# Shared-key attention: key tiles summed four at a time on GpSimd before the ones product

## The chip, the cores and the metric

The kernel runs on one core of one Trainium2 chip. The metric is the device time of one execution in microseconds (us). Five engines work side by side and meet only at semaphores: TensorE (PE, with its weight loads shown apart as PEld), VectorE (DVE), ScalarE (ACT), GpSimd (POOL) and SyncE (SP), which issues most DMAs.

## The reference

Two sandwich layers on a sequence of 2 x 2048 tokens of 128 values: local attention, a feed-forward layer, causal attention, a second feed-forward layer. The change lies in the attention inside the first feed-forward layer. It has four query heads of 32 dimensions that share one set of keys and values, over all 2048 tokens of a batch:

```
Q = (nx @ Wq.T).reshape(B, S, H, dk).transpose(0, 2, 1, 3)
Kc = nx @ Wkc.T
Vc = nx @ Wvc.T
scores = jnp.einsum('bhsd,btd->bhst', Q, Kc) * scale
attn = jax.nn.softmax(scores, axis=-1)
out = jnp.einsum('bhst,btd->bhsd', attn, Vc)
```

The softmax needs for each query and head the sum of 2048 exponentials. That sum is what the change works out in another way.

## The kernel before

The function is mqa_attention, L761 to L1253. The queries of a batch are cut into 8 units of 256 (UQ); there are 16 units, U0 to U7 in batch 0 and U8 to U15 in batch 1. The 2048 keys are cut into 16 tiles of 128 (KT), taken two at a time; gi = 0 to 7 counts these pairs within a unit.

For each unit and each key tile:
- TensorE multiplies keys with the four heads' queries (scores, L1170) into PSUM.
- ScalarE takes the exponential (L1049) into one of six slots of the ring pt: 128 keys by 4 heads by 256 queries. It waits until the slot's last readers are done: the values product of tile T - 6 and the GpSimd add that read it (sums_with, L830, counts the adds that must be done).
- TensorE multiplies values with the exponentials (values, L1181), four matmuls of 32 columns each, one a head, adding up in the bank pvb.
- For the denominators, GpSimd adds the exponentials of two tiles (L1089) into one of three buffers psum, seven such pair sums a unit. TensorE then multiplies a matrix of ones with each pair sum (sums, L1189), again four matmuls, adding up in the other half of pvb. The last two tiles of a unit are not added first: TensorE multiplies ones with each of them (last_sums, L1196). That is nine products with ones a unit.

Before a unit's exponentials can be taken, its row maxima must be known. They are found a unit or two ahead, in 32 passes (first_pass, L1154, with VectorE's maximum at L914), laid between the other work by the tables EARLY, LATE and ALL. At gi = 5 (TURN) VectorE closes the next unit's maxima in top (L917): a reduction over the 32 partial maxima (L919), a cast of the result into the tile mt (L924) and a subtraction for its low part (L926). TensorE waits for these and turns mt round (max_rows, L1160), and ScalarE and VectorE copy the rows out (L1025, L931). Ahead of max_rows TensorE projects the queries of the unit after the next (project, L64 to L66). Unit U6 of a batch has no such projection, and U7 has neither passes nor maxima.

At the end of a unit (close, L1201) TensorE does the last two values products, the last pair sum and last_sums. ScalarE then evacuates pvb (L1032), TensorE turns it (L1211), and VectorE divides (post, L939 and L941). The first scores of a unit are queued on TensorE behind the close of the one before.

The order on each engine is that of the code. On TensorE at each gi: two scores, at gi = 5 the projection and max_rows, some passes, the values of the pair before, the pair sum of gi - 2, some passes. Between units some engines do other small work: VectorE statistics, weights or normalised rows for the next stage (L716 to L724, L1874, L1883, L963), GpSimd powers (L735, L1078) and two subtractions (L1895). S.stats and later are these helpers.

Of the kernel before, what the change touches and what calls it, by code (L numbers as in the profile page):

```python
# [9 lines left out]
ALU = mybir.AluOpType  # L10
# [718 lines left out]
def stats_pool(nc, pool, S, rows=slice(0, 2), chunks=range(4)):  # L729

    n = rows.stop - rows.start
    for c in chunks:
        tiles = slice(c * S.CT, (c + 1) * S.CT)
        pool.wait_ge(S.step, 1 + (c + 1) * S.chunk_steps)
        nc.gpsimd.tensor_tensor(S.rs[:, rows, tiles], S.ve[:, rows, tiles],  # L735
                                S.half[:, 0:n * S.CT].rearrange("p (a b) -> p a b", b=S.CT),
                                ALU.pow).then_inc(S.powed, 1)
# [10 lines left out]
KT = SEQ // P  # L748
# [4 lines left out]
RING = 6  # L753
UQ = 256
UT = UQ // P
SUMS = 3
PAIR_SUMS = KT // 2 - 1
GRP = 4


def mqa_attention(nc, dr, X, g, S, wq, wkv, ao, later, x2):  # L761

    m = Mem(nc, "b1_")
    with m:
# [8 lines left out]
        pt = m.sb("pt", [P, RING, HB, UQ])  # L773
        psum = m.sb("psum", [P, SUMS, HB, UQ])
# [33 lines left out]
        summed = m.sem("summed")  # L808
        den_mm = m.sem("den_mm")
        st_mm = m.sem("st_mm")  # L810
        exp_done = m.sem("exp_done")
# [17 lines left out]

        def sums_with(T):  # L830

            return T // KT * PAIR_SUMS + min(T % KT // 2 + 1, PAIR_SUMS)

        def block_of(U):
            return U % UNITS
# [9 lines left out]
        def passes_at(u, g, half):  # L845

            if g >= TURN:
                return (u + 2, EARLY[g][half]) if u + 2 < UNITS else (None, 0)
            if u + 1 >= UNITS:
                return None, 0  # L850
            return u + 1, (ALL if u == 0 else LATE)[g][half]

        with nc.Block() as block:
# [210 lines left out]
            @block.gpsimd  # L1064
            def _(pool):
                nc.gpsimd.memset(ones[:, :], 1.0).then_inc(zeroed, 1)
                nc.gpsimd.memset(mt[:, :, :], 0.0).then_inc(zeroed, 1)
                pool.wait_ge(zeroed, 2)
                nc.gpsimd.memset(ks[QROWS:QROWS + 2, :].bitcast(F32), 1.0).then_inc(zeroed, 1)
                pool.wait_ge(zeroed, 3)  # L1070

                def between(U):
                    if U in (2, 3):
                        stats_pool(nc, pool, S, rows=slice(1, 2), chunks=(U,))
                    if U in (4, 5):
                        half = slice(BT * (U - 4), BT * (U - 3))
                        pool.wait_ge(S.step, 1 + S.CHUNKS * S.chunk_steps)
                        nc.gpsimd.tensor_tensor(S.r[:, half], S.ve[:, 0, half], S.half[:, half], ALU.pow).then_inc(r_done, 1)  # L1078
                    if U in (6, 7):
                        later.low2(nc, pool, U - 6)  # L1080

                for U in range(BATCH * UNITS):
                    between(U)
                    for k in range(PAIR_SUMS):
                        T, n = U * KT + 2 * k, U * PAIR_SUMS + k
                        pool.wait_ge(exp_done, T + 2)
                        if n >= SUMS:
                            pool.wait_ge(den_mm, n - SUMS + 1)
                        nc.gpsimd.tensor_tensor(psum[:, n % SUMS, :, :], pt[:, T % RING, :, :], pt[:, (T + 1) % RING, :, :],  # L1089
                                                ALU.add).then_inc(summed, 1)  # L1090

            @block.tensor
            def _(pe):
# [19 lines left out]
                def load(b):  # L1113
                    turn_in(b, 0)
                    turn_in(b, 1)
                    for i in range(BB):
                        n = b * BB + i
                        cols = slice(i * BLK, (i + 1) * BLK)
                        if i + 2 < BB:
                            turn_in(b, i + 2)  # L1120
                        pe.wait_ge(xh_ready, n + 1)
                        pe.wait_ge(xl_ready, n + 1)
                        if i >= 2:
                            pe.wait_ge(k_lo, n - 1)
                        matmul_split(nc, p1b[:, i % 2, :], wkv[0][:, :], wkv[1][:, :], xh[:, cols],
                                     xl[:, cols]).then_inc(kv_mm, 1)
                        if i > 0:
                            turn_values(b, i - 1)
                    turn_values(b, BB - 1)
                    pe.wait_ge(k_lo, (b + 1) * BB)  # L1130
                    pe.wait_ge(v_ready, (b + 1) * BB)
# [25 lines left out]
                def max_rows(V):  # L1157
                    pe.wait_ge(m_split, V * 2 + 2)
                    for t in range(UT):
                        last = nc.tensor.transpose(misc[:, t * P:(t + 1) * P], mt[:, t, :], ident[:, :])  # L1160
                    last.then_inc(mt_mm, 1)
# [13 lines left out]
                def values(U, i):  # L1175
                    T = U * KT + i
                    if i == 0 and U > 0:
                        pe.wait_ge(post_done, U)
                    pe.wait_ge(exp_done, T + 1)
                    for h in range(HB):  # L1180
                        last = nc.tensor.matmul(pvb[h * DK:(h + 1) * DK, 0:UQ], v1[:, i, :], pt[:, T % RING, h, :],  # L1181
                                                start=(i == 0), stop=(i == KT - 1), skip_group_check=True)
                    last.then_inc(pv_mm, 1)

                def sums(U, k):
                    n = U * PAIR_SUMS + k
                    pe.wait_ge(summed, n + 1)
                    for h in range(HB):
                        last = nc.tensor.matmul(pvb[h * DK:(h + 1) * DK, UQ:2 * UQ], ones[:, :], psum[:, n % SUMS, h, :],  # L1189
                                                start=False, stop=False, skip_group_check=True)  # L1190
                    last.then_inc(den_mm, 1)

                def last_sums(U):
                    for i in (KT - 2, KT - 1):
                        for h in range(HB):
                            last = nc.tensor.matmul(pvb[h * DK:(h + 1) * DK, UQ:2 * UQ], ones[:, :],  # L1196
                                                    pt[:, (U * KT + i) % RING, h, :], start=False, stop=(i == KT - 1),
                                                    skip_group_check=True)
                    last.then_inc(den_last, 1)

                def close(U):  # L1201
                    values(U, KT - 2)
                    values(U, KT - 1)
                    sums(U, PAIR_SUMS - 1)
                    last_sums(U)

                def post(U):
# [7 lines left out]
                for b in range(BATCH):  # L1215
                    load(b)
                    V = b * UNITS
                    project(V)
                    for r in range(P1):
                        first_pass(V, r)  # L1220
                    max_rows(V)
                    project(V + 1)
                    done = [0] * UNITS
                    for u in range(UNITS):
                        U = V + u

                        def passes(g, half):
                            w, count = passes_at(u, g, half)
                            for _ in range(count):
                                first_pass(V + w, done[w])  # L1230
                                done[w] += 1

                        for gi in range(PAIRS_OF_TILES):
                            if gi == 0 and u > 0:
                                close(U - 1)
                            scores(U, 2 * gi)
                            scores(U, 2 * gi + 1)
                            if gi == TURN and u + 2 < UNITS:
                                project(U + 2)
                            if gi == TURN and u + 1 < UNITS:  # L1240
                                max_rows(U + 1)
                            passes(gi, 0)
                            if gi == 0 and u > 0:
                                post(U - 1)
                            if gi > 0:
                                values(U, 2 * gi - 2)
                                values(U, 2 * gi - 1)
                            if gi > 1:
                                sums(U, gi - 2)
                            passes(gi, 1)  # L1250
                    close(U)
                    post(U)
                    pe.wait_ge(post_done, (b + 1) * UNITS)  # L1253
# [2215 lines left out]
```

## Time and profile before

| | us |
|---|---|
| Median of 3 runs | 2171.54 |
| Lowest and highest run | 2165.57, 2171.64 |
| Profiled execution, first to last instruction (span) | 2116.7 |
| The two together: the median less the span | 54.8 |

The page gives the profiled execution's own time as its span, 2116.7 us; the time of a run also holds what lies around the span. Busy shares of the span:

| Engine | busy us | share |
|---|---|---|
| TensorE matmuls | 1765.5 | 83% |
| TensorE weight loads | 1331.8 | 63% |
| VectorE | 1492.7 | 71% |
| ScalarE | 974.9 | 46% |
| GpSimd | 923.7 | 44% |

A matmul of float32 data shows as two records, so the four matmuls of one product with ones are eight records. Matmuls are pipelined and their ends modelled, so the distance from one start to the next says more than a duration. The granted clock of TensorE is 1.00 at 2.4 GHz and 0.50 at 1.2 GHz. The stage that changes runs from 640 to 1177 us of the span, with the loading of batch 1 in the middle (884 to 933).

### The profile page before, as it was taken

The page shows a single profiled execution, that of the slowest core. Times are in us where ns is not written, and L with a number is a line of the kernel's source. Part 1 is how long each engine was busy: PE and PEld are TensorE (multiplying, and loading weights), DVE is VectorE, ACT ScalarE, POOL GpSimd, SP SyncE. Part 2 cuts the span into 40 slices and gives each one's busy share as a digit, 9 for nine tenths or more (in the row PEclk, how much of TensorE's full clock was granted, in tenths as well). Part 3 has the DMA queues.
Part 4 walks back from the last instruction along what each step waited for, and adds up shares of the span by engine and source line. Part 5 has one row for each costly group of instructions (what it writes and reads, how often), then busy time and mean ns, then how long its engine had stood idle before and what let it go on. Part 6 is the DMA issues. An engine that isn't in the chain of part 4 may idle for free. (4 is left out here: it accounts for less than half of the span.)

```text
span 2116.7 us, 37485 instructions
## 1 busy us (share of the span) xinstructions
PE 1765.5 (83%) x13932; PEld 1331.8 (63%) x13932; DVE 1492.7 (71%) x3418; ACT 974.9 (46%) x2147; POOL 923.7 (44%) x637
## 2 busy tenths in 40 slices
PE   3788888888769999889999779965899779978993
PEld 2677777777635666446665557644688558767883
DVE  5678777787477887387787478878787776864234
ACT  2455545545415565525556345432333244325664
POOL 3455555565314566514555336654000220165644
PEclk9999999999859999979999889988899889988997
DMA  5112112111010000000000023319600000016763
GB/s 172 66 63 81 51 71 76 56 71 66 16 42 1 2 1 1 1 1 1 1 2 1 1 71 101 95 60 229 149 1 1 0 1 1 8 38 194 213 219 118
DMA packets 78469, 124.11 MB, mean 59 GB/s; under 512 B 11824, under 2 KB 43440, under 8 KB 77776
## 3 DMA queue, kind: packets, MB, share of 16 engines
q1 hardware_dynamic: 73744, 112.31, 17.1%
q0 software_dynamic: 4544, 9.41, 1.3%
q8 instruction: 111, 1.82, 0.4%
q14 instruction: 70, 0.57, 0.1%
HBM read 59.19 MB, written 28.94 MB: 42 GB/s over the span
## 5 line engine op out<-in xcount | busy, mean ns | idle before, releaser
L1089 POOL TENSOR_TENSOR mb_psum<-mb_pt 128x1024 f32<-128x1024 f32 x112 | 267.0, 2387 | 291.4 <-ACT mb_pt L1049 290.5
L1049 ACT ACTIVATE mb_pt<-mb_stb 128x1024 f32<-128x1024 f32 x256 | 249.2, 1021 | 143.2 <-PE mb_stb L1170 142.7
L914 DVE TENSOR_REDUCE mb_mxp<-mb_p1b 128x1 f32<-128x512 f32 x352 | 231.2, 684 | 50.2 <-PE mb_p1b L1154 46.3
L351 DVE TENSOR_TENSOR ma_tr<-ma_pbank,ma_cs 128x512 f32<-128x512 f32 x256 | 161.7, 683 | 91.4 <-PE ma_pbank L66 81.6
L488 ACT ACTIVATE ma_e<-ma_sbank,ma_mx 128x80 f32<-128x80 f32 x512 | 120.3, 385 | 99.0 <-DVE ma_mx L358 99.0
L2466 PE MATMUL mc_pv<-mc_pt,mc_v 128*128 128x256 f32 x544 | 148.2, 398 | 17.3 <-DVE mc_pt L2269 17.3
L1154 PE MATMUL mb_p1b<-mb_ks,mb_qs 96*128 96x512 f32 x352 | 151.3, 473 | 7.0 <-DVE mb_qs L907 3.3
L439 POOL TENSOR_TENSOR ma_qt<-ma_tr,ma_swp 128x512 f32<-128x512 f32 x64 | 82.3, 1289 | 167.8 <-DMA ma_swp<-ma_tr 167.7
L1170 PE MATMUL mb_stb<-mb_qs,mb_ks 98*128 98x512 f32 x512 | 143.8, 402 | 0.8 <-ACT mb_pt L1049 0.8
L2269 DVE COPY mc_pt<-mc_tb 128x512 f32<-128x512 f32 (+1 forms) x144 | 94.0, 658 | 61.5 <-PE mc_tb L2451 61.1
L1181 PE MATMUL mb_pvb<-mb_pt,mb_v 128*32 128x256 f32 x2048 | 137.0, 385 | 0.0
L1593 POOL TENSOR_TENSOR mb_hh<-mb_hh,mb_gb 128x512 f32<-128x512 f32 x64 | 98.7, 1545 | 82.8 <-DVE mb_hh L1610 55.4
L1756 POOL TENSOR_TENSOR mc_frs<-mc_fve,mc_half 128x4 f32<-128x4 f32 x8 | 8.1, 1012 | 275.5 <-DVE mc_fve L1740 275.4
L914 DVE TENSOR_REDUCE mb_mxp<-mb_misc 128x1 f32<-128x512 f32 x160 | 109.2, 682 | 22.0 <-PE mb_misc L1154 22.0
L2466 PEld LDWEIGHTS mc_pv<-mc_pt,mc_v 128*128 128x128 f32 x544 | 96.8, 196 | 35.3 <-DVE mc_pt L2269 25.8
L1170 PEld LDWEIGHTS mb_stb<-mb_qs,mb_ks 98*128 98x128 f32 x512 | 94.2, 189 | 33.2 <-issue 12.3
L498 ACT ACTIVATE ma_pt<-ma_fbank 128x512 f32<-128x512 f32 (+1 forms) x160 | 94.2, 590 | 42.2 <-PE ma_fbank L605 41.8
L64 PE MATMUL ma_pbank<-ma_xth,ma_wh 128*128 128x256 f32 x256 | 85.6, 334 | 30.0 <-DVE ma_tr L351 30.0
L1154 PEld LDWEIGHTS mb_p1b<-mb_ks,mb_qs 96*128 96x128 f32 x352 | 67.4, 199 | 67.8 <-DVE mb_mxp L914 48.2
L448 POOL TENSOR_TENSOR ma_pb<-ma_e,ma_rden 64x1024 f32<-64x1024 f32 x32 | 90.1, 2817 | 31.6 <-DVE ma_rden L367 31.6
L613 PE MATMUL ma_fbank<-ma_pt,ma_v 128*64 128x128 f32 x1024 | 73.6, 287 | 35.3 <-ACT ma_pt L498 35.2
L441 POOL TENSOR_TENSOR ma_kt<-ma_tr,ma_swp 128x512 f32<-128x512 f32 x64 | 83.6, 1316 | 39.0 <-DMA ma_swp<-ma_tr 34.6
(404 smaller groups left out, 4767.2 us busy)
## 6 DMA issues: line engine op xcount, KB each, us to landing
ma_swp<-ma_tr SPq DMA_DIRECT2D x256, 128.0 KB, 2.0
md_wslot<-d_weights SPq DMA_DIRECT2D x39, 516.0 KB
d_xs<-mw_blank SPq DMA_DIRECT2D x1, 16899.0 KB, 72.3
mb_gb<-b_gates SPq DMA_DIRECT2D x64, 256.0 KB, 3.2
md_xs<-d_xs SPq DMA_DIRECT2D x39, 131.0 KB, 3.3
md_work<-d_ret SPq DMA_DIRECT2D x8, 512.0 KB, 5.4
mg_X<-x SPq DMA_DIRECT2D x4, 512.0 KB, 9.8
ma_cs<-cs SPq DMA_DIRECT2D x1, 2048.0 KB, 9.9
```

What stands on the lines that cost most here:

```text
L351: nc.vector.tensor_tensor(tr[:, G % TRS, part, :, :], pbank[:, i % 2, :].rearrange("p (c t) -> p c t", c=2), cs[:, b // 2, part, None, :]. ...
L488: nc.scalar.activation(e[:, s, slot, :], sbank[:, 2 * j + k // 4, k % 4 * KEYS0:(k % 4 + 1) * KEYS0], ACT.Exp, bias=mx[:, s, slot:slot + 1 ...
L498: nc.scalar.activation(to[:, 4 * q:4 * q + nh, :], filled_bank(a, s, i)[:, 0:nh * P].rearrange("p (a b) -> p a b", b=P), ACT.Copy).then_in ...
L914: nc.vector.tensor_reduce(mxp[:, r // NCH, r % NCH:r % NCH + 1], pass_bank(r), AXX, ALU.max).then_inc(p1_max, 1)
L1049: nc.scalar.activation(pt[:, T % RING, :, :].rearrange("p (b h) q -> p b (h q)", b=2), stb[:, 2 * (i % 2):2 * (i % 2) + 2, :], ACT.Exp, sc ...
L1089: nc.gpsimd.tensor_tensor(psum[:, n % SUMS, :, :], pt[:, T % RING, :, :], pt[:, (T + 1) % RING, :, :], ALU.add).then_inc(summed, 1)
L1154: nc.tensor.matmul(pass_bank(r), qs[V % 3][0:QROWS, h, t * P:(t + 1) * P], ks[0:QROWS, c * BLK:(c + 1) * BLK], start=True, stop=True).then ...
L1170: last = nc.tensor.matmul(stb[:, 2 * (i % 2) + hp, :], ks[:, i * P:(i + 1) * P], qs[U % 3][:, 2 * hp:2 * hp + 2, :].rearrange("p h q -> p ...
L1181: last = nc.tensor.matmul(pvb[h * DK:(h + 1) * DK, 0:UQ], v1[:, i, :], pt[:, T % RING, h, :], start=(i == 0), stop=(i == KT - 1), skip_gro ...
L1593: nc.gpsimd.tensor_tensor(hh[:, t % HR, :], hh[:, t % HR, :], gb[:, q % GBR, :], ALU.mult).then_inc(gated, 1)
L2269: nc.vector.tensor_copy(pt[:, K % 2, 0:wd], tb[:, K % 2, 0:wd]).then_inc(pt_copied, 1)
L2466: last = nc.tensor.matmul(pv[:, 0:HC * P], v[:, t, :], pt[:, K % 2, a * HC * P:(a + 1) * HC * P], start=(t == 0), stop=(t == r))
```

## The change

GpSimd now adds four tiles instead of two. Three times a unit it adds a tile pair into a buffer, then adds the third and the fourth tile to that buffer in place, each add waiting for the one before it. Tiles 12 and 13 are added as a pair, as before, and tiles 14 and 15 still go to TensorE singly. So GpSimd makes 10 adds a unit, not 7 (ADDS), and TensorE multiplies ones with 4 sums (SUMS_PER_UNIT) and 2 single tiles, not 7 and 2. The product of a quad comes at gi = 3, 5 and 7, that of the last pair in close. The ring of six slots and the three sum buffers stay as they are.

```
-PAIR_SUMS = KT // 2 - 1
+QUADS_OF_TILES = 3
+ADDS = 3 * QUADS_OF_TILES + 1
+SUMS_PER_UNIT = QUADS_OF_TILES + 1
...
-            return T // KT * PAIR_SUMS + min(T % KT // 2 + 1, PAIR_SUMS)
+            return T // KT * ADDS + min(3 * (T % KT // 4) + max(T % 4, 1), ADDS)
...
-                    for k in range(PAIR_SUMS):
-                        T, n = U * KT + 2 * k, U * PAIR_SUMS + k
+                    for j in range(SUMS_PER_UNIT):
+                        T, n = U * KT + 4 * j, U * SUMS_PER_UNIT + j
+                        total = psum[:, n % SUMS, :, :]
                         pool.wait_ge(exp_done, T + 2)
                         if n >= SUMS:
                             pool.wait_ge(den_mm, n - SUMS + 1)
-                        nc.gpsimd.tensor_tensor(psum[:, n % SUMS, :, :], pt[:, T % RING, :, :], pt[:, (T + 1) % RING, :, :],
+                        nc.gpsimd.tensor_tensor(total, pt[:, T % RING, :, :], pt[:, (T + 1) % RING, :, :],
                                                 ALU.add).then_inc(summed, 1)
+                        if j < QUADS_OF_TILES:
+                            for i in (2, 3):
+                                pool.wait_ge(exp_done, T + i + 1)
+                                pool.wait_ge(summed, U * ADDS + 3 * j + i - 1)
+                                nc.gpsimd.tensor_tensor(total, total, pt[:, (T + i) % RING, :, :],
+                                                        ALU.add).then_inc(summed, 1)
...
-                def sums(U, k):
-                    n = U * PAIR_SUMS + k
-                    pe.wait_ge(summed, n + 1)
+                def sums(U, j):
+                    n = U * SUMS_PER_UNIT + j
+                    pe.wait_ge(summed, U * ADDS + min(3 * j + 3, ADDS))
...
-                    sums(U, PAIR_SUMS - 1)
+                    sums(U, SUMS_PER_UNIT - 1)
...
-                            if gi > 1:
-                                sums(U, gi - 2)
+                            if gi >= 3 and gi % 2 == 1:
+                                sums(U, (gi - 3) // 2)
```

## Rows read from the trace of the kernel before

**Rows 1.** The page: the span, and each engine's busy us, share and instructions.

```profile
span 2116.7 us, 37485 instructions
PE 1765.5 (83%) x13932; PEld 1331.8 (63%) x13932; DVE 1492.7 (71%) x3418; ACT 974.9 (46%) x2147; POOL 923.7 (44%) x637
```

**Rows 2.** The page's costliest groups: count | busy, mean ns | idle before, its releaser.

```profile
L1089 POOL TENSOR_TENSOR mb_psum<-mb_pt 128x1024 f32<-128x1024 f32 x112 | 267.0, 2387 | 291.4 <-ACT mb_pt L1049 290.5
```

**Rows 3.** Timeline of ScalarE, L1032 (start us, us; idle before): starts of U2, U5, U6, U7, and U7's end.

```profile
708.41 0.60 ACT L1032 ACTIVATE mb_ots<-mb_pvb 128x512 f32<-128x512 f32 x1 [3.40 <-PE mb_pvb L1196]
...
802.54 0.60 ACT L1032 ACTIVATE mb_ots<-mb_pvb 128x512 f32<-128x512 f32 x1 [3.40 <-PE mb_pvb L1196]
...
833.96 0.60 ACT L1032 ACTIVATE mb_ots<-mb_pvb 128x512 f32<-128x512 f32 x1 [3.40 <-PE mb_pvb L1196]
...
861.96 0.60 ACT L1032 ACTIVATE mb_ots<-mb_pvb 128x512 f32<-128x512 f32 x1 [2.14 <-PE mb_pvb L1196]
...
883.92 0.60 ACT L1032 ACTIVATE mb_ots<-mb_pvb 128x512 f32<-128x512 f32 x1 [2.15 <-PE mb_pvb L1196]
```

**Rows 4.** Busy time by stretch, U7: length, then PE, PEld, DVE, ACT, POOL, clock.

```profile
861.96:883.92 21.96, 21.49 (x236) 11.45 (x236) 0.63 (x2) 16.60 (x19) 16.57 (x7) 1.00 0.01 1
```

**Rows 5.** Timeline of TensorE in U7.

```profile
865.25 1.07 PE L1181 MATMUL mb_pvb<-mb_pt,mb_v 128*32 128x256 f32 x16
866.25 1.21 PE L1170 MATMUL mb_stb<-mb_qs,mb_ks 98*128 98x512 f32 x4
867.39 1.07 PE L1181 MATMUL mb_pvb<-mb_pt,mb_v 128*32 128x256 f32 x16
...
868.83 1.20 PE L1170 MATMUL mb_stb<-mb_qs,mb_ks 98*128 98x512 f32 x4
```

**Rows 6.** Timeline of GpSimd: first adds of U2 and U7, and two memsets.

```profile
711.53 4.73 POOL L1089 TENSOR_TENSOR mb_psum<-mb_pt 128x1024 f32<-128x1024 f32 x2
...
864.61 11.94 POOL L1089 TENSOR_TENSOR mb_psum<-mb_pt 128x1024 f32<-128x1024 f32 x5 [3.38 <-ACT mb_pt L1049]
...
590.47 0.31 POOL L1067 MEMSET mb_mt<- 128x256 f32 x1
590.84 1.80 POOL L1069 MEMSET mb_ks<- 2x2048 f32 x1
```

**Rows 7.** Timeline of TensorE's weight loads: the last pair sum of U7.

```profile
882.16 0.35 PEld L1189 LDWEIGHTS mb_pvb<-mb_psum,mb_ones 128*32 128x32 f32 x8
```

**Rows 8.** Timeline of U15; for L963, L1883 counts, min/median/max ns, first and last start.

```profile
1157.57 9.40 POOL L1089 TENSOR_TENSOR mb_psum<-mb_pt 128x1024 f32<-128x1024 f32 x4 [4.89 <-ACT mb_pt L1049]
...
L963 DVE TENSOR_SCALAR mb_x<-mg_X,mb_mean,mb_rs x2: 341/1412/2484, 1157.3 to 1157.6; 128x128 f32<-128x128 f32 x2
...
L963 DVE TENSOR_SCALAR mb_x<-mg_X,mb_mean,mb_rs x2: 2419/2452/2484, 1157.6 to 1160.0; 128x128 f32<-128x128 f32 x2
...
L1883 DVE TENSOR_TENSOR mb_w<-mbw_r,mb_w x4: 751/758/2347, 832.9 to 1031.6; 128x576 fp32r<-128x576 f32 x4
```

**Rows 9.** Timelines of VectorE, GpSimd and TensorE at gi = 5 of U5; TensorE in U6.

```profile
820.64 0.19 DVE L919 TENSOR_REDUCE mb_negm<-mb_mxp 128x8 f32<-128x32 f32 x1
820.86 0.18 DVE L924 CAST mb_mt<-mb_negm 128x8 fp32r<-128x8 f32 x1
821.07 0.18 DVE L926 TENSOR_TENSOR mb_mt<-mb_negm,mb_mt 128x8 fp32r<-128x8 f32 x1
...
823.94 2.40 POOL L1089 TENSOR_TENSOR mb_psum<-mb_pt 128x1024 f32<-128x1024 f32 x1 [3.03 <-ACT mb_pt L1049]
...
822.16 0.38 PE L1160 MATMUL mb_misc<-mg_ident,mb_mt 128*128 128x128 f32 x2
...
852.74 0.44 PE L1160 MATMUL mb_misc<-mg_ident,mb_mt 128*128 128x128 f32 x2 [0.87 <-DVE mb_mt L926]
```

**Rows 10.** Busy time by stretch, behind U7; columns as in rows 4.

```profile
884.00:888.00 4.00, 2.33 (x11) 1.40 (x11) 2.69 (x10) 1.11 (x2) 0.00 (x0) 1.00 0.01 2
888.00:892.00 4.00, 3.01 (x9) 1.64 (x8) 2.75 (x7) 1.19 (x2) 0.00 (x0) 0.51 0.00 0
```

## The prediction

> **What bounds the kernel now.** I read the page first. The profiled execution's span is 2116.7 us, and the runs shown have a median of 2171.54 us, so some 54.8 us lie outside the span; I take them as unchanged. TensorE is busy 83% of the span, VectorE 71%, GpSimd 44% [rows 1]. The change touches one stage, some 535 us long: 16 units (8 a batch), in which 112 pair sums of 2387 ns leave GpSimd idle for as long again [rows 2]. So next I looked at the unit boundaries, which are ScalarE's evacuations at L1032 [rows 3]. An ordinary unit (U5) takes 31.42 us. The next to last of a batch (U6) takes 28.00 us. The last (U7), with no maxima to work out, takes 21.96 us. TensorE is busy 21.49 of those 21.96 us, at full clock [rows 4]. TensorE is the bound in each of these units.
>
> Below, E is a unit's start (its evacuation row), and times are counted from it. Batch 1 (U8 to U15) repeats batch 0.
>
> **TensorE's gain.** Three of the nine sums go from each unit: those in tile pairs gi = 2, 4 and 6. In U7 the step from one pair's values to the next scores is 1.00 us without a sum (865.25 to 866.25) and 1.44 us with one (867.39 to 868.83) [rows 5]: 0.44 us a sum, 1.33 us a unit, 21.3 us over 16 units if nothing else moved.
>
> **GpSimd's cost.** Seven adds a unit become ten, and six of the ten wait for the add ahead of them. Two independent adds in a row took 4.73 us, so the second starts 2.34 us after the first [rows 6]. The trace has no dependent add. The nearest row is a memset that waits for one of GpSimd's own: it starts 0.06 us after that one's end (590.47 + 0.31, then 590.84) [rows 6]. I take 2.387 + 0.06 = 2.45 us from start to start. The bounds are 2.34 us (the wait costs nothing) and 2.60 us (a generous 0.2 us for wait and restart). Ten adds then take 3 x (2.45 + 2.45 + 2.34) + 2.39 = 24.1 us from the first start. The first starts at E + 2.65 in U7 (861.96 to 864.61), after evacuation and two exponentials, and at E + 3.12 in U2 and U3, which first have a power op there (708.41 to 711.53) [rows 3, 6]. The last add ends at E + 26.8, and the next unit's evacuation is 1.76 us behind the start of the last sum on TensorE (882.16 to 883.92) [rows 3, 7]. So no unit can be shorter than 26.8 + 0.05 + 1.76 = 28.6 us.
> - U7 and U15, now 21.96 us: 28.6, a loss of 6.6 us each, 13.3 us together. TensorE has 1.33 us less to do there and waits for GpSimd at each sum.
> - U6 and U14, now 28.00 us: this limit alone would cost 0.6 us each.
> - Other units: 31.42 - 1.33 = 30.1 us, above 28.6, so this limit doesn't bite. In them the first quad is complete at about E + 9.9 and the second at E + 17.2, ahead of TensorE's turn for them.
>
> Without another effect the sum is 12 x (-1.33) + 2 x 0.6 + 13.3 = -1.5 us. GpSimd's adds were hidden where TensorE has its maxima work, and have no cover in the two last units.
>
> **What a busy GpSimd does to VectorE.** In U15 seven tensor_scalar ops from SBUF to SBUF meet GpSimd's adds. Alone such an op takes 0.34 us; one that began at 1157.6, when an add began, took 2.484 us, until that add's end, and one behind it took 2.419 us, while four adds ran back to back in 9.40 us [rows 8]. So one such op gets through for each end of an add. A tensor_tensor with two SBUF inputs (L1883) took 0.751 us or, beside an add, 2.347 us [rows 8]. A tensor_reduce doesn't wait: in U5 L919 took 0.19 us at 820.64, inside the add that ended at 820.91 [rows 9]. A rule agrees with this: the Trainium skill, SBUF — State Buffer, Who interferes with whom, has tensor_copy, cast and tensor_scalar (in a two-port mode) and a tensor_tensor with both inputs in SBUF blocked for the whole of a GpSimd instruction that started first, and tensor_reduce never. By that page both L924 and L926 below are of the kinds that block.
>
> On the path to TensorE there are two such ops: at gi = 5 VectorE closes the next unit's maxima by L919 (reduce), L924 (a cast from SBUF to SBUF) and L926 (two SBUF inputs), and max_rows (L1160) on TensorE waits for the last. Behind that wait stand, in order on TensorE, the values and sums of gi = 5, the passes, and the scores of tiles 12 and 13, and so ScalarE and GpSimd as well. Now L924 and L926 fall in a pause of GpSimd: in U5 they start at 820.86 and 821.07 and take 0.18 us each; GpSimd's next add begins at 823.94 after 3.03 us idle, so the one before was over at 820.91 [rows 9]. After the change GpSimd has no pause there. Its sixth add (index 5) ends at 2.65 + 14.5 = E + 17.2, the next at 19.5, the next at 22.0. L924 was asked for at E + 18.32 and comes 0.88 us sooner (two sums gone): E + 17.44. That is 0.25 us too late for the end at 17.2, so it waits till 19.5; L926 comes about 0.2 us later, finds the next add begun, and waits till 22.0. Max_rows start at 22.25 instead of 19.62 - 0.88 = 18.74 [rows 9]: TensorE stands for 3.5 us. From max_rows to the unit's end were 31.42 - 19.62 = 11.80 us, now 11.36.
> - U1, U4, U5, U9 to U13 (8 units): 22.25 + 11.36 = 33.6 us, +2.2 each, 17.6 us.
> - U2 and U3 (adds start at 3.12, so ends at 17.6 and 20.0): L924 catches 17.6, L926 waits to 20.0, end 31.6, +0.3 each, 0.6 us.
> - U0 and U8: their exponentials come late and GpSimd has pauses; L924 waits for the add of tile 10 and L926 gets in ahead of tile 11. A stall of about 1.5 us against 1.33 gained: +0.2 each, 0.4 us.
> - U6 and U14: max_rows at 22.25; from there to the end were 861.96 - 852.74 = 9.22 us [rows 3, 9], now 8.78: 31.0, +3.0 each (in place of the 0.6 above), 6.0 us.
> - U7 and U15 have no such step: 13.3 us as above.
>
> Sum: 17.6 + 0.6 + 0.4 + 6.0 + 13.3 = +37.9 us. For each of these terms the lower bound is that neither op waits and the upper one a full add more (+2.4 us).
>
> **TensorE's clock.** Stalls of 3.5 us are new in this stage, where the clock is 1.00. After the stretch from 884 to 888, in which TensorE was busy 2.33 of 4 us, the clock is 0.51, the 1.2 GHz level [rows 10]. Four us of work at that level would cost up to 2 us. Over the ten units with a long stall that is 0 to 20 us. I take 5 us, since part of a slow stretch falls into the stall itself.
>
> **Edits costed at nothing.** Ring: exponential T waits for the add that read tile T - 6, which is done 2 us or more before in every unit with maxima, and in U7 GpSimd sets the pace anyway. The three sum buffers: an add waits for a sum three before, long consumed. L735 and L1078 on GpSimd stand between units, in the pause from E - 3 on, behind evacuation and the first exponentials; if that were gone each would cost its 1.6 to 2.9 us once. The in-place form of the adds is taken at the price of the others; between -0.05 and +0.25 us each in 24 adds of four GpSimd-bound units that is -1 to +6 us.
>
> **Forecast and rivals.**
> - A, forecast (0.50): both ops wait in turn as above. +38 + 5 = +43 us: 2171.5 + 43 = 2214.5, span about 2160. Its own range is 2203 to 2226.
> - B (0.15): the chain of adds is 0.06 us or more slower per dependent add, so L924 catches the sixth add's end in the eight units. Max_rows start at 20.1, the unit ends at 31.5 (+0.03), U6 and U14 at 28.9 (+0.9): 0.2 + 0.6 + 0.4 + 1.8 + 13.3 = +16 us, 2188. For it: the margin is a quarter of a us. Against: the rows' 0.06 us.
> - C (0.12): only one of the two waits (the small copy doesn't, or both slip through one gap). Max_rows at 19.8 give -0.3 in eight units, +0.6 in U6 and U14, -1.3 in U2 and U3, 13.3 at the end: +10 us, 2181. For it: no row shows ops of 8 elements with stride beside an add.
> - D (0.10), the other side: VectorE's small ops don't contend at all. Then TensorE's 16 us come home in twelve units and the two last units eat them: -1.5 us, 2170. It decides if L924 and L926 stay at 0.17 us beside a busy GpSimd. Against: the long rows of L963 and L1883.
> - E (0.05): as D, and GpSimd keeps up in U7 (dependent adds faster than 2.34 us, or fewer of them on the path): down to -15 us, 2157. Nothing in the rows speaks for it.
> - F (0.08): as A, but the clock falls behind each stall and in the gaps of U7 too: 20 us for it instead of 5, and 2 us in U7 and U15: 2171.5 + 38 + 20 + 4 = 2233.
>
> The range of 2176 to 2231 leaves out D, E and part of F. A measurement of this kernel can tell about 0.3% (6.5 us) from no change. Slower by more: A, B, C and F, 0.85. Within 0.3%: D, 0.10. Faster: E, 0.05.
>
> **What the profile after would show.** L1189 has 512 matmul records instead of 896, and GpSimd 160 adds of about 2.39 us, start to start 2.45 where dependent. U7 lasts 28.6 us, with TensorE waiting at sums for GpSimd. The mean of L924 rises from 0.17 to about 1.5 to 2 us and of L926 to about 2 us in the units with maxima; TensorE waits 3 to 4 us for L926 at L1160; U5 lasts 33.6 us and U6 31.0. I am wrong if L924 and L926 stay short (D), if their waits sum to one add rather than two (B, C), or if U7 stays under 26 us (E).

## The result and the profile after

The changed kernel takes 2190.27 us (median of 4 runs, 2186.98 to 2198.28), the kernel before 2170.86 (4 runs). The ratio of the two kernels' runs is 1.0099, with a 95% interval of 1.0081 to 1.0117: slower by 19 us by the medians and by 21 us by the ratio. That is slower, as forecast, and inside the range, but only about half of the 43 us of the forecast.

The first two rows of the page after, and GpSimd's two groups of adds (count | busy, mean ns | idle before, its releaser):

```profile
span 2185.2 us, 36813 instructions
PE 1763.3 (81%) x13548; PEld 1321.0 (60%) x13548; DVE 1517.7 (69%) x3418; ACT 976.0 (45%) x2147; POOL 1038.0 (48%) x685
L1098 POOL TENSOR_TENSOR mb_psum<-mb_psum,mb_pt 128x1024 f32<-128x1024 f32 x96 | 229.1, 2386 | 19.4 <-ACT mb_pt L1051 6.8
L1092 POOL TENSOR_TENSOR mb_psum<-mb_pt 128x1024 f32<-128x1024 f32 x64 | 152.2, 2378 | 182.5 <-ACT mb_pt L1051 182.3
```

GpSimd makes 160 adds of 2.38 us where it made 112 [rows 2], the in-place ones at the same price.

The two profiled spans, 2116.7 us [rows 1] and 2185.2, must not be subtracted. This profiled execution took 2186.98 us, so only 1.8 us lie outside its span. The 54.8 us that I took for time outside the span were a difference between executions: later runs of the kernel before had a median of 2121 us on some chips and 2168 on another. 49 us of the two spans' difference lie behind the stage that was changed, in code that is the same. So I compare stages: from the first memset (L1066 before, 590.4 us) to the last evacuation (1176.9) it took 586.5 us before, 587.5 in a second profile of that kernel on a slower chip (run e9), and 608.5 after: +22.0 us. Even so, two stretches of the stage differ between executions of the same code: U0 with its load took 86.6 and 86.8 us in the two profiles of the kernel before and 85.1 to 87.8 in the others, and U8 with its load 85.2 to 87.9. Unit times are steadier.

Busy time by stretch of the kernel after, for U5, U6, U7 and two stretches in U6: length, then PE, PEld, DVE, ACT, POOL, clock.

```profile
800.98:832.53 31.55, 29.98 (x259) 18.32 (x260) 26.65 (x43) 18.63 (x23) 24.99 (x11) 1.00 0.00 1
832.53:863.85 31.32, 28.18 (x237) 16.12 (x238) 19.09 (x30) 17.43 (x21) 25.49 (x11) 0.89 0.00 1
863.85:892.54 28.69, 22.91 (x212) 10.68 (x212) 0.63 (x2) 16.59 (x19) 23.56 (x10) 0.94 0.00 1
...
850.00:854.00 4.00, 1.40 (x10) 0.69 (x14) 3.15 (x4) 1.73 (x4) 3.86 (x3) 0.66 0.00 0
854.00:858.00 4.00, 4.00 (x28) 1.83 (x24) 1.38 (x2) 0.91 (x2) 3.48 (x2) 0.50 0.00 0
```

The three units were 31.42, 28.00 and 21.96 us [rows 3]. In U7, TensorE stands for 5.8 of 28.69 us, while GpSimd is busy for 23.56 us with its ten adds. In U6 the granted clock falls to the 1.2 GHz level behind a stretch in which TensorE worked 1.40 of 4 us.

Units in us, from evacuation to evacuation, of every kernel (ordinary units are U1 to U5 and U9 to U13):

| | U1 | U2 | U5 | U6 | U7 | U14 | U15 | stage |
|---|---|---|---|---|---|---|---|---|
| before | 31.44 | 31.35 | 31.42 | 28.00 | 21.96 | 27.97 | 21.95 | 586.5 |
| after | 31.55 | 31.80 | 31.55 | 31.32 | 28.69 | 30.38 | 28.81 | 608.5 |
| e5 (after again) | 31.51 | 31.79 | 31.52 | 31.31 | 28.69 | 29.03 | 28.79 | 606.8 |
| e1 row in PSUM | 30.13 | 30.14 | 30.12 | 29.12 | 28.68 | 28.94 | 28.80 | 592.5 |
| e2 pairs in last units | 31.54 | 31.83 | 31.55 | 27.94 | 21.91 | 27.99 | 21.96 | 589.1 |
| e3 both | 30.10 | 30.14 | 30.17 | 27.97 | 21.95 | 28.00 | 21.96 | 574.4 |
| e4 four adds | 30.15 | 30.16 | 30.10 | 27.14 | 21.14 | 27.16 | 21.14 | 568.4 |
| e6 before, row in PSUM | 31.38 | 31.43 | 31.44 | 28.01 | 21.89 | 28.01 | 21.89 | 587.0 |
| e7 adds 1 us later | 32.30 | 34.36 | 33.95 | 29.11 | 28.69 | 29.03 | 28.79 | 623.8 |
| e8 that, row in PSUM | 30.13 | 30.28 | 30.12 | 29.14 | 28.68 | 28.90 | 29.72 | 588.6 |
| e10 best | 30.07 | 30.10 | 30.07 | 27.11 | 21.90 | 27.11 | 21.89 | 569.2 |

Now the step at gi = 5. In the code after, the cast is L926, the subtraction L928, max_rows L1169, a first add L1092 and a chained one L1098. Timelines of VectorE, GpSimd and TensorE in U5 (start us, us; a count of 2 is two instructions in a row), then of U3, where the first line gives the cast by its count, min/median/max ns and start:

```profile
818.42 2.42 DVE L926 CAST mb_mt<-mb_negm 128x8 fp32r<-128x8 f32 x1
820.87 0.17 DVE L928 TENSOR_TENSOR mb_mt<-mb_negm,mb_mt 128x8 fp32r<-128x8 f32 x1
...
803.63 2.39 POOL L1092 TENSOR_TENSOR mb_psum<-mb_pt 128x1024 f32<-128x1024 f32 x1 [3.78 <-ACT mb_pt L1051]
...
813.55 4.92 POOL L1098 TENSOR_TENSOR mb_psum<-mb_psum,mb_pt 128x1024 f32<-128x1024 f32 x2
818.43 2.37 POOL L1092 TENSOR_TENSOR mb_psum<-mb_pt 128x1024 f32<-128x1024 f32 x1
820.95 4.91 POOL L1098 TENSOR_TENSOR mb_psum<-mb_psum,mb_pt 128x1024 f32<-128x1024 f32 x2
...
821.10 0.44 PE L1169 MATMUL mb_misc<-mg_ident,mb_mt 128*128 128x128 f32 x2 [1.25 <-DVE mb_mt L928]
```

```profile
L926 DVE CAST mb_mt<-mb_negm x1: 517/517/517, 755.1 to 755.1; 128x8 fp32r<-128x8 f32 x1
755.66 2.29 DVE L928 TENSOR_TENSOR mb_mt<-mb_negm,mb_mt 128x8 fp32r<-128x8 f32 x1
...
755.55 2.35 POOL L1092 TENSOR_TENSOR mb_psum<-mb_pt 128x1024 f32<-128x1024 f32 x1
758.05 4.90 POOL L1098 TENSOR_TENSOR mb_psum<-mb_psum,mb_pt 128x1024 f32<-128x1024 f32 x2
```

In U5 the cast meets the start of an add (818.43) and takes 2.42 us instead of 0.18 [rows 9]: the whole add. The subtraction behind it takes 0.17 us. It begins at 820.87, between that add's end and the start of the next (820.95), which waits for the one before it. I wrote ahead of the prediction that the engines meet only at semaphores; no semaphore ties these two ops to GpSimd's adds, and still they wait. In U3 it is the other way round: the cast waits 0.35 us for an add's end, the next add is independent and starts at once, and the subtraction waits all of it, 2.29 us. Over the 16 units (count: min/median/max ns, first and last start):

```profile
L926 DVE CAST mb_mt<-mb_negm x16: 175/2372/2415, 633.1 to 1154.5; 128x8 fp32r<-128x8 f32 x16
L928 DVE TENSOR_TENSOR mb_mt<-mb_negm,mb_mt x16: 174/175/2292, 633.3 to 1156.9; 128x8 fp32r<-128x8 f32 x16
```

The cast waits a full add in 12 of the 16, the subtraction in two alone (U2 and U3). In the profiles of after, e5 and e7 together, the subtraction got through in all 22 units where the cast had waited out an add and a chained add came next, and waited out an add in all 14 where the next one was independent. (U0 and U8, where GpSimd pauses behind the add, are not counted.) Why a chained add leaves the gap is not shown beyond its later start.

### The profile page after: what moved, and what is told of

Read it like the earlier page. It is cut to its first block and busy times, and to the rows that moved or that the text cites. A ratio compares the mean times of both kernels' runs of the same rounds, so it can differ in the third digit from the quotient of the medians.

```text
span 2185.2 us, 36813 instructions
## 1 busy us (share of the span) xinstructions
PE 1763.3 (81%) x13548; PEld 1321.0 (60%) x13548; DVE 1517.7 (69%) x3418; ACT 976.0 (45%) x2147; POOL 1038.0 (48%) x685
## 3 DMA queue, kind: packets, MB, share of 16 engines
HBM read 59.19 MB, written 28.94 MB: 40 GB/s over the span
## 5 line engine op out<-in xcount | busy, mean ns | idle before, releaser
L1092 POOL TENSOR_TENSOR mb_psum<-mb_pt 128x1024 f32<-128x1024 f32 x64 | 152.2, 2378 | 182.5 <-ACT mb_pt L1051 182.3
L1098 POOL TENSOR_TENSOR mb_psum<-mb_psum,mb_pt 128x1024 f32<-128x1024 f32 x96 | 229.1, 2386 | 19.4 <-ACT mb_pt L1051 6.8
L1179 PE MATMUL mb_stb<-mb_qs,mb_ks 98*128 98x512 f32 x512 | 148.6, 412 | 0.8 <-ACT mb_pt L1051 0.8
L3118 POOL DMA_INDIRECT d_ret<-md_ys,md_home x78 | 77.0, 987 | 74.5 <-DVE md_ys L3251 60.8
L64 PE MATMUL ma_pbank<-ma_xth,ma_wh 128*128 128x256 f32 x256 | 85.1, 333 | 30.1 <-DVE ma_tr L351 30.0
L3332 PE MATMUL md_bk<-md_xT,md_wslot 128*128 128x256 f32 x312 | 97.9, 399 | 12.7 <-ACT md_a L3062 8.1
```

Of the source, the lines that this page charges most:

```text
L1092: nc.gpsimd.tensor_tensor(total, pt[:, T % RING, :, :], pt[:, (T + 1) % RING, :, :], ALU.add).then_inc(summed, 1)
L1098: nc.gpsimd.tensor_tensor(total, total, pt[:, (T + i) % RING, :, :], ALU.add).then_inc(summed, 1)
L1179: last = nc.tensor.matmul(stb[:, 2 * (i % 2) + hp, :], ks[:, i * P:(i + 1) * P], qs[U % 3][:, 2 * hp:2 * hp + 2, :].rearrange("p h q -> p ...
L3332: nc.tensor.matmul(ub[:, c, :], wslot[:, j % WRING, c * P:(c + 1) * P], xT[:, j % 2, :], start=True, stop=True).then_inc(up_mm, 1)
```

## The experiments

**e1: the contention alone.** The reduced maxima go to a free corner of the PSUM bank misc, so that the cast has no SBUF input and the subtraction only one.

```
-        negm = m.sb("negm", [P, HB, UT])
...
-                    nc.vector.tensor_reduce(negm[:, :, :].rearrange("p h t -> p (h t)"), mxp[:, :, :], AXX, ALU.max,
+                    nc.vector.tensor_reduce(misc[:, BLK - HB * UT:BLK], mxp[:, :, :], AXX, ALU.max,
...
-                    nt = negm[:, :, :].rearrange("p h t -> p t h")
+                    nt = misc[:, BLK - HB * UT:BLK].rearrange("p (h t) -> p t h", t=UT)
```

> The changed kernel, with the 8 maxima a partition that the cast and the subtraction read kept in PSUM (a free corner of the bank misc) and not in SBUF, so that neither op has two SBUF inputs nor goes from SBUF to SBUF; GpSimd's ten adds stay. Theory (the stall at gi = 5 is VectorE's wait for GpSimd's running add): both ops take about 0.2 us, TensorE's wait at max_rows goes back to under 1 us, U5 falls from 31.55 to 30.1 us, U6 from 31.3 to 28.8, U7 stays at 28.7: 12 x (-1.33) + 2 x 0.8 + 13.6 = -1 us against the kernel before, about 2170 us. Rival (TensorE waits for GpSimd's slower sums and for the ring, the VectorE wait is beside it): U5 stays at 31.5, the kernel at 2190 us.

2121.05 us, kernel before 2121.06: ratio 0.9995 (0.9977 to 1.0014). Timelines of e1 in U5:

```profile
819.10 0.17 DVE L925 CAST mb_mt<-mb_misc 128x8 fp32r<-128x8 f32 x1
819.30 0.17 DVE L927 TENSOR_TENSOR mb_mt<-mb_misc,mb_mt 128x8 fp32r<-128x8 f32 x1
...
819.09 2.38 POOL L1091 TENSOR_TENSOR mb_psum<-mb_pt 128x1024 f32<-128x1024 f32 x1
...
820.38 0.38 PE L1168 MATMUL mb_misc<-mg_ident,mb_mt 128*128 128x128 f32 x2
```

Both ops run inside an add at full speed, max_rows wait for nothing, and the unit takes 30.12 us, 1.4 less than after. This agrees with the Trainium skill, SBUF — State Buffer, Who interferes with whom: a VectorE op with at most one SBUF input, outside the two-port modes, doesn't contend. The stage is 608.5 - 592.5 = 16 us shorter than after. By units it is more: 14.7 us in the ten ordinary ones, which are the waits, and 3.6 us in U6 and U14, where after had two falls of the clock; U0 and U8 with their loads took 2.3 us longer. U7 stays at 28.68: the other loss is of another kind. U6 ends at 29.12 us with the clock at 1.00, not at 28.0, since its two last sums now wait for GpSimd:

```profile
857.00 0.16 PEld L1197 LDWEIGHTS mb_pvb<-mb_psum,mb_ones 128*32 128x32 f32 x8 [1.50 <-POOL mb_psum L1097]
...
859.31 0.16 PEld L1197 LDWEIGHTS mb_pvb<-mb_psum,mb_ones 128*32 128x32 f32 x8 [1.29 <-POOL mb_psum L1091]
```

**e2: the last units alone.** Units U6 and U7 of a batch keep the seven pairs; semaphore counts follow the plan.

```
+FOURS = [4, 4, 4, 2]
+PAIRS_ALL = [2] * 7
+PLAN = [FOURS] * 6 + [PAIRS_ALL] * 2
...
-                    for j in range(SUMS_PER_UNIT):
+                    for g in PLAN[U % len(PLAN)]:
```

> The changed kernel, with the old seven pair sums in U6, U7, U14 and U15 alone (quads in the other twelve units). Theory (GpSimd's ten adds are the bound where no maxima cover them): U7 goes back to 22.0 us and U6 to 28.0; what stays are the +0.1 to +0.45 us of the twelve other units, some +2 us: 2190.3 - 19 = about 2171 to 2173 us. Rival (as the forecast had it, most of the loss is VectorE's wait in the units with maxima): 13 us come back at most, 2177 us or more.

2120.77 us, ratio 1.0011 (0.9993 to 1.0028). ScalarE's evacuations at the ends of U4 to U7:

```profile
802.44 0.60 ACT L1051 ACTIVATE mb_ots<-mb_pvb 128x512 f32<-128x512 f32 x1 [3.40 <-PE mb_pvb L1227]
833.99 0.60 ACT L1051 ACTIVATE mb_ots<-mb_pvb 128x512 f32<-128x512 f32 x1 [3.40 <-PE mb_pvb L1227]
861.93 0.60 ACT L1051 ACTIVATE mb_ots<-mb_pvb 128x512 f32<-128x512 f32 x1 [2.14 <-PE mb_pvb L1227]
883.84 0.60 ACT L1051 ACTIVATE mb_ots<-mb_pvb 128x512 f32<-128x512 f32 x1 [2.14 <-PE mb_pvb L1227]
```

U6 and U7 are back at 27.94 and 21.91 us. The stage is 19.4 us shorter than after, so each of the two edits alone gives back most of the 22 us: the rival, by which 13 us come back at most, falls.

**e3: both edits.**

> Both edits: maxima row in PSUM, and pair sums in the two last units of each batch. Theory (two separate costs, and a TensorE gain of 1.33 us in each of twelve units): 2170.9 - 16 = 2155 us, U5 30.1, U6 28.0, U7 22.0 us. Rival (the two edits mend one and the same wait): no better than the better of the two alone, 2170 us.

2106.31 us, ratio 0.9942 (0.9917 to 0.9966): 12.3 us faster by the ratio. The stage is 34.1 us shorter than after. Without U0 and U8 it is 33.9 us, and e1 gave 14.7 in the ordinary units, e2 19.4 in the last ones: they add up, U6 and U14 counted once. What is left is TensorE's own gain, 1.25 us in each of ten ordinary units. The 16 us that I expected for the stage were missed, it is 12.1: the stretch that loads batch 1 and computes U8 took 87.89 us here and 86.08 before, where 84.7 were expected. That stretch took 85.2 to 87.9 us over all runs, at a mean granted clock of 0.71 to 0.78; what decides this stays open.

**e4: no chained adds.** The two chained adds of each quad are left out, with the semaphore counts to match, so GpSimd makes four adds a unit and the denominators lack six of sixteen tiles.

```
-                        if j < QUADS_OF_TILES:
-                            for i in (2, 3):
-                                pool.wait_ge(exp_done, T + i + 1)
-                                pool.wait_ge(summed, U * ADDS + 3 * j + i - 1)
-                                nc.gpsimd.tensor_tensor(total, total, pt[:, (T + i) % RING, :, :],
-                                                        ALU.add).then_inc(summed, 1)
```

> TensorE's gain by itself: as the changed kernel, but GpSimd makes only the first add of each quad and the last pair's (4 adds a unit, not 10), so the denominators leave out six of sixteen tiles. Theory: TensorE sets the pace in every unit and gains 1.33 us in each: 2170.9 - 21.3 = 2149.6 us, U5 30.1 and U7 20.6 us. Rival (VectorE's maxima or the exponentials take over as the bound once sums go): less than half of it, above 2160 us.

2099.86 us, ratio 0.9906 (0.988 to 0.9931). Every unit is short: 30.1, 27.14, 21.14 us. So TensorE's saving exists wherever GpSimd keeps up, and the loss lies in the chained adds alone. In U6 and U7 only 0.86 and 0.82 of the 1.33 us came. Timelines of e4 in U7, TensorE's scores and their weight loads behind a pair without a sum:

```profile
861.67 1.37 PE L1173 MATMUL mb_stb<-mb_qs,mb_ks 98*128 98x512 f32 x4
...
862.30 0.30 PEld L1173 LDWEIGHTS mb_stb<-mb_qs,mb_ks 98*128 98x128 f32 x2 [0.34 <-ACT mb_pt L1051]
```

Behind such a pair the scores now wait for ScalarE's exponentials, and the step from scores to values takes 1.30 us (861.67 to 862.97) instead of 1.12 behind a pair with a sum in the kernel before (868.83 to 869.95). Three such steps give back 0.5 of U7's 1.33 us: the rival, that exponentials become the bound, holds in part there.

**e5: the changed kernel again.** No edit.

> The changed kernel once more, beside the kernel before on the chip of these runs (in the runs above the kernel before had a median of 2121 us, 50 us under that of the first comparison). Theory (the loss lies in fixed waits of the attention stage): +19 to +22 us again, a ratio of 1.009 to 1.010, U5 31.55 us, U7 28.7 us. Rival (part of the loss belonged to the execution or chip of the first comparison, where the time behind the stage differed by 50 us): a ratio under 1.006.

2140.72 us, before 2120.73: ratio 1.011 (1.0079 to 1.0141). On a chip that runs the kernel before in 2121 us the loss is 20 us, as on one of 2170, and the two ratios (1.0099 and 1.011) agree within their intervals.

**e6: the kernel before, with its row in PSUM.** The edit of e1 on the kernel before.

> Control for the edit of the first experiment: the kernel before, with the 8 maxima in PSUM and nothing else changed. Theory (in the kernel before the cast and the subtraction fall in a pause of GpSimd): no change, ratio 1.000, U5 31.4 us. Rival (the edit gains by itself, by quicker reads): faster by 0.2 us a unit or more, 3 us in all.

2120.85 us, ratio 1.0003 (0.9983 to 1.0023). Without a busy GpSimd the edit does nothing; what it gives in e1 is the contention that the change brought.

**e7: adds a microsecond later.** If what an op pays depends on which add ends beside it, shifting the adds against VectorE must bring the second wait in U1 to U5. An idle memset (1.06 us) goes ahead of those units' first add.

```
+        idle = m.sb("idle", [P, 1152])
...
+                        if j == 0 and U % UNITS in (1, 2, 3, 4, 5):
+                            nc.gpsimd.memset(idle[:, :], 0.0)
```

> The changed kernel, with one more op on GpSimd, a memset of some 1.2 us, ahead of the first add in U1 to U5 and U9 to U13: the adds of these ten units run 1.2 us later and are over long before TensorE would need them. Theory (an end of an independent add lets one of the two small VectorE ops through, an end with a dependent add behind it lets both through): the cast is asked for at E + 17.4, waits for the sixth add's end at 18.7, the subtraction then waits for the whole seventh to 21.1: TensorE stands for 2.4 us, U5 goes from 31.55 to 32.6 us, ten units cost 11 us more than in the changed kernel, a ratio of 1.014 to 1.015. Rival (one wait a unit, whatever the phase): the cast waits 1.25 us in place of 2.4, and U5 gets faster, 30.4 us.

2161.78 us, ratio 1.0203 (1.0169 to 1.0236). Timelines of e7 in U1, then TensorE and two stretches in U4, and one stretch in U3:

```profile
693.56 1.02 DVE L927 CAST mb_mt<-mb_negm 128x8 fp32r<-128x8 f32 x1
694.62 2.27 DVE L929 TENSOR_TENSOR mb_mt<-mb_negm,mb_mt 128x8 fp32r<-128x8 f32 x1
...
694.50 2.35 POOL L1095 TENSOR_TENSOR mb_psum<-mb_pt 128x1024 f32<-128x1024 f32 x1
697.00 4.90 POOL L1101 TENSOR_TENSOR mb_psum<-mb_psum,mb_pt 128x1024 f32<-128x1024 f32 x2
...
797.91 0.44 PE L1172 MATMUL mb_misc<-mg_ident,mb_mt 128*128 128x128 f32 x2 [1.96 <-DVE mb_mt L929]
...
796.00:800.00 4.00, 2.09 (x22) 1.05 (x26) 3.91 (x5) 2.24 (x4) 3.86 (x2) 0.79 0.00 0
800.00:804.00 4.00, 4.00 (x32) 2.32 (x28) 2.13 (x5) 1.45 (x2) 2.69 (x2) 0.78 0.00 0
...
764.00:768.00 4.00, 3.95 (x29) 1.85 (x30) 2.17 (x5) 0.75 (x2) 3.75 (x2) 0.57 0.00 0
```

The cast now catches the sixth add's end, and the subtraction meets an independent add and waits for all of it, as in U3 after. The rival (one wait, and a faster unit) falls. The loss is larger than expected: the ten units took 19.4 us more than in e5, not 11, and the clock has the larger part in that. U1, U9 and U10 took 32.3 us, with a mean granted clock of 1.00. U4, U5 and U11 to U13 took 33.9, and U2 and U3, whose adds begin 0.5 us later still, 34.3: in these seven the clock fell behind max_rows' stall, to a mean of 0.95. Units with nearly the same stall (1.92 to 2.00 us) differ by 1.6 us with and without the fall, so seven falls cost some 11 us (an estimate).

**e8: e7 with the row in PSUM.**

> The same late adds with the maxima row in PSUM, as control. Theory: without VectorE's waits the later adds cost next to nothing, U5 30.1 to 30.4 us, some 0 to 3 us over the first experiment: ratio 1.000 to 1.002. Rival (the later adds delay TensorE's sums or the ring, and that is what the kernel with late adds pays): U5 above 31 us here too.

2118.38 us, ratio 0.9989 (0.9968 to 1.001). The late adds cost nothing (U1 to U5 30.1 to 30.3 us) once VectorE's two ops wait for no add: the whole of e7's loss in these units was the waits and the clock behind them. (U15 took 29.72 us at a mean clock of 0.89, where it took 28.79 at 1.00 in e7; what brought the clock down there stays open.)

**e9: the kernel before, one look.**

> One look at the kernel before, for a second profile of it. The load of batch 1 with U8 took 86.1 us in the first profile of before, and 85.3 to 87.9 us in the kernels with quads, where 84.7 us were expected. Theory (what TensorE's clock does in the load differs between executions of any kernel): it lies apart from 86.1 by 1 us or so here too. Rival (the quads bring the slow load with them): 86.1 us again.

2169.93 us against 2168.24 (11 runs). Its units agree with the first profile's to 0.1 us, and its load of batch 1 with U8 took 86.54 us against 86.08. Kernels with quads lie on both sides of these (85.2 to 87.9). The expected difference of 1 us was 0.5, so the run decides little: that quads make this stretch slower in some runs isn't excluded.

**e10: the best version.** As e3, but U6 has quads where they fit:

```
-PLAN = [FOURS] * 6 + [PAIRS_ALL] * 2
+PLAN = [FOURS] * 6 + [[4, 4, 2, 2, 2], PAIRS_ALL]
```

> The version the other runs point to: maxima row in PSUM; quads in six units a batch, in U6 two quads and three pairs (nine adds), in U7 the seven pairs. Theory: U6 goes from 28.0 to 27.1 us (two sums less for TensorE, and GpSimd's nine adds end by E + 26.1), the rest as in the third experiment: -14 us against before, ratio 0.9935. Rival (nine adds are too many for U6): U6 28.0 us or more, and no gain over the third experiment's 0.9942.

2156.44 us, before 2168.24: ratio 0.9944 (0.9924 to 0.9964). Evacuations at the ends of U5, U6 and U7:

```profile
826.74 0.60 ACT L1050 ACTIVATE mb_ots<-mb_pvb 128x512 f32<-128x512 f32 x1 [3.40 <-PE mb_pvb L1226]
853.85 0.60 ACT L1050 ACTIVATE mb_ots<-mb_pvb 128x512 f32<-128x512 f32 x1 [2.14 <-PE mb_pvb L1226]
875.75 0.60 ACT L1050 ACTIVATE mb_ots<-mb_pvb 128x512 f32<-128x512 f32 x1 [2.15 <-PE mb_pvb L1226]
```

U6 is 0.9 us shorter than in e3. Over both batches this is too little to tell e10 from e3 in total time. Both beat the kernel before by about 12 us and, by the ratios of different chips (0.994 against 1.010 and 1.011), the changed one by about 35. The stage of e10 is 18.3 us shorter than in e9, on the same chip: 5 us of that are lost again behind the stage, where the code is the same (994.3 us in e10's profile, 989.4 in e9's). Their cause stays open.

## Why the prediction was partly right, and the step that failed

In stage times, the forecast's terms against what they measured:

| term | forecast | measured |
|---|---|---|
| U1, U4, U5, U9 to U13 | 17.6 | 1.3 |
| U2, U3 | 0.6 | 0.9 |
| U0, U8 | 0.4 | 0.6 |
| U6, U14, clock at full speed | 6.0 | 2.1 |
| U7, U15 | 13.3 | 13.6 |
| clock | 5 | 3.6 |
| sum | 43 | 22 |

(U0 and U8 hold the loads, which differ by more than 0.6 us between executions.)

- **TensorE's gain** was right in the ordinary units: 1.33 us a unit forecast, 31.42 - 30.12 = 1.30 in e1's U5. In U6 and U7 it is 0.8 to 0.9 us (e4), which changes nothing here, since GpSimd sets the pace there.
- **GpSimd's limit in U7 and U15** was right: 28.6 us forecast, 28.69 and 28.81 measured, and e2 gave all of it back. The chained adds cost a little more than I took: a dependent one starts 820.95 - 818.43 = 2.52 us behind the add ahead of it, not 2.45, and an independent one (4.88 - 2.52) 2.36 us. Last rows of GpSimd and TensorE in U7 after: the last add, and the sum that waits for it, with the evacuation 1.57 us later.

```profile
888.55 2.36 POOL L1092 TENSOR_TENSOR mb_psum<-mb_pt 128x1024 f32<-128x1024 f32 x1
...
890.97 0.16 PEld L1198 LDWEIGHTS mb_pvb<-mb_psum,mb_ones 128*32 128x32 f32 x8 [1.30 <-POOL mb_psum L1092]
```

- **That the cast waits for a whole add** was right, to its place: asked at E + 17.44 in forecast and trace, gone 2.42 us later.
- **The step that failed** is the next one: "L926 comes about 0.2 us later, finds the next add begun, and waits till 22.0". It didn't find it begun. The eighth add depends on the seventh and starts 0.14 us or so behind its end, and in that gap the subtraction got in (820.87 against 820.95). Max_rows started at E + 20.12, not 22.25. From there to the unit's end were 11.43 us (forecast 11.36), so the unit was 31.55 and not 33.6. I had priced the gap at 0.06 us for GpSimd's own time and not asked who else gets in there. Rows 8 show one op for each end of an add, but those adds are all independent. This is the second half of rival C, "both slip through one gap". C's sum (+10) was too low by the later end (19.8 forecast, 20.12 measured), by U2 and U3, where only one op slips through, and by the clock. e7 tests the reading the other way: with an independent add next, the subtraction waits.
- **U6 and U14** carry the same error. With the clock up, such a unit takes 29.0 us (U14 in e5 and e7), +1.0 and not +3.0. It takes as long without the waits (29.12 and 28.94 in e1), so GpSimd's limit alone, for which I had 0.6, costs this 1.0 us. In the profile after, both had a fall of the clock: 31.32 and 30.38 us, together 3.6 us more. I had spread 5 us for the clock over all units with a stall; in the ordinary ones the stall is 1.25 us in place of 3.5, and the clock stays at 1.00, as in U5's row.
- **D and E** fell with the cast's 2.42 us, and **F** with the clock in U1 to U5. **B**'s condition came true (a dependent add is 0.07 us slower than I took), but the cast still misses the sixth add's end, by next to nothing: it comes at 818.42, the seventh add starts at 818.43. B's times (max_rows at 20.1, the unit 31.5, U6 28.9) are nevertheless those measured (20.12, 31.55, 29.0): both ways end at the seventh add. That is luck of the numbers and doesn't bear out B; U5's rows and e7 do tell them apart.
- **The time outside the span** (54.8 us) was wrong, without harm to the difference.

By the experiments the stage's sum is: TensorE's gain in the ten ordinary units -12.5 (e3); VectorE's waits there +14.6 (after against e3); the four last units +19.3, of them 13.6 GpSimd's adds in U7 and U15, 2.1 in U6 and U14 and 3.6 the clock; U0 and U8 +0.6. Together that is +22.0, as measured. That the measured time still lay in the range is owed to the range's width, not to the mechanism: the terms for the ordinary units were 16 us too high.

## What to carry to other kernels

Idle time of a third engine isn't free to use: ask whom its instructions lock out, and in which stages the cover is gone. Here a 0.17 us op on the critical path cost 1.4 us a unit beside a busy GpSimd, and moving its 8-element operand to PSUM took that away. Where stages of a loop differ in their bound, give each its own plan (quads where TensorE has maxima to work on, pairs in the last units), since one plan for all can lose at the end what it wins before.

## What was unexpected of the hardware

- What a small VectorE op pays beside back-to-back GpSimd adds hangs on whether the next add is dependent: if the next add waits on GpSimd's own semaphore, the cast and the subtraction (0.17 us) both get through behind one add (U5); if it is independent, only the first does (0.52, then 2.29 us, U3).
- Stalls of TensorE at max_rows of up to 1.44 us (by the matmul's row) left the clock at 1.00 in all ten ordinary units after. In e7 stalls of 1.95 us were followed by a fall, at some 1.6 us, and one of 2.00 us wasn't (U10); U14's stall of 3.03 us was in after and wasn't in e5. So the length of the stall alone doesn't decide it.
- One program on one core differs by 2.2% between chips (2121 and 2168 us), and nearly all of it lies outside the stage studied here (two profiles of the kernel before: spans 51.4 us apart, stages 1.0).
